# Second experts layer: weighted outputs summed slot by slot into the output, all shared tiles ahead of the slots

## The chip, the cores and the metric

The kernel runs as one program on one core of a Trainium2 chip. The metric is the device time of one execution in microseconds (us). Before the change the median of 3 runs is 1013.5 us (1013.17 to 1015.44). The profiled execution, from which all rows below come, took 1014.64 us, of which the trace spans 1012.9 us.

## The reference, cut to what matters

The program computes two layers, each cross attention followed by a mixture of experts, on 16 x 128 = 2048 tokens of 256 values. The change is in the last stage, the second mixture:

```python
shared = new_gelu(xf @ Wfc_s + bfc_s) @ Wproj_s + bproj_s
topk_p, topk_i = jax.lax.top_k(softmax(xf @ Wr), 2)
topk_p = topk_p / jnp.sum(topk_p, axis=-1, keepdims=True)
gate = jnp.zeros((N, 8)).at[jnp.arange(N)[:, None], topk_i].add(topk_p)
for e in range(8):
    h = new_gelu(xf @ Wfc[e] + bfc[e]) @ Wproj[e] + bproj[e]
    routed = routed + h * gate[:, e:e + 1]
x = x + shared + routed
```

Here xf is the layer norm of x, each expert has a hidden width of 1024, and each token goes to two of the eight experts. A shared expert of the same size takes every token. The first mixture has 14 experts of width 512 and no shared one.

## The kernel before

The kernel is written engine by engine: each engine's program is one list in the order in which the code is written, and semaphores tie the lists together. A stage ends with a barrier of all engines (`end_phase`). Tokens stand in 16 tiles of 128; `c["X"]` holds the running sum of all tiles in SBUF, `c["Hn"]` their layer norm.

**The stage `shared_expert`** does two things at once. TensorE takes tiles 0 to 13 (`SHARED_FIRST` = 14) through the shared expert: `turn` transposes a tile, `up` makes 8 chunks of 128 hidden values, `down` brings them back to 256 outputs, and VectorE adds these to X (L1698). Meanwhile VectorE builds the routing table: each of the 4096 pairs (token, expert) gets a place in one of 39 slots of 128 rows, where a slot belongs to one expert. `mark_places` and `mark_slots` write one-hot rows for each of 32 chunks, TensorE multiplies them in tiles 2 to 9 (L1432), and `slot_rows` turns the product into `src` (which token row a slot's row reads) and `dst` (where its output row goes). Rows of slots that no token fills read some row and write to a pad row. SyncE loads the weights of all eight experts, 16 MB, in this stage.

**The stage `experts`** runs over the 39 slots; it is used by both layers (45 slots in the first). GpSimd gathers a slot's 128 token rows with an indirect DMA (L1455), four slots ahead. TensorE transposes them, runs `up` for slot n+1, then `turn` for n+2, then `down` for n. VectorE copies the slot's first weights into the ring `wp` (L1924, two copies a slot in the second layer), copies the transposed rows (L1916), and adds the expert's bias to the output into `yb` (L1936). GpSimd scatters `yb` with an indirect DMA to the tensor `token_outputs` in HBM (L1776), where each pair has a row of its own. Slots 0 and 1 and the last ones are written out, the others run in a loop of two slots a turn.

**The end of the second layer.** After slot 38 TensorE takes the shared tiles 14 and 15 in the same pipeline (L1813, L1821, L1829). When all scatters have landed, SyncE loads for each tile the two rows of each token (L1759). VectorE multiplies both by the token's weights `w12` and adds them to X for tiles 0 to 9 (L1950, L1953); ScalarE multiplies (L1907) and GpSimd adds (L1797) for tiles 10 to 15. SyncE stores each tile to the output (L1765) and waits for all 16 stores.

Two orders matter below. On GpSimd the list is gather(n+4), scatter(n), with scatter waiting for `yb` and gather for a transpose. On VectorE each slot's bias add reads the expert's number into a register first, after the wait for the output:

```python
dve.wait_ge(y_done, n + 1)
if after(n, 2):
    dve.wait_ge(y_stored[par], 16 * k)
e = dve.value_load(routing["expert"][0:1, at(n)], min_val=0, max_val=E - 1)
```

Of the kernel before, what the change touches and what calls it, by code (L numbers as in the profile page):

```python
# [13 lines left out]
P = 128  # L14
B = 16
# [12 lines left out]
SHARED_FIRST = 14  # L28
CHUNK = 4
AHEAD = 4  # L30
ON_DVE = 10
LOAD_ORDER = (0, 10, 1, 2, 11, 3, 4, 12, 5, 6, 13, 7, 14, 8, 9, 15)
STORE_ORDER = (0, 1, 10, 2, 11, 3, 4, 12, 5, 13, 6, 7, 14, 8, 9, 15)
# [20 lines left out]
def build(nc, a, out):  # L54

    with ExitStack() as top:
# [39 lines left out]
        c["kv_stored"] = [nc.alloc_semaphore(f"kv_stored{i}") for i in range(2)]  # L96
        c["hn_stored"] = [nc.alloc_semaphore(f"hn_stored{layer}") for layer in range(2)]
# [34 lines left out]
        shared_expert(nc, sem, alloc, c, moe1, routing, weights, shared)  # L132
        end_phase()
        experts(nc, sem, alloc, c, moe1, routing, weights, shared, out)
# [1075 lines left out]
def table(keep, moe):  # L1210

    return {
        "w12": keep("w12", [P, B, TOPK]),
        "src": keep("src", [P, moe.slots], I32),
        "dst": keep("dst", [P, moe.slots], I32),
        "expert": keep("expert", [P, moe.slots], I32),
    }
# [56 lines left out]
def route_buffers(sb, moe, weights):  # L1274
# [3 lines left out]
    return {  # L1278
# [11 lines left out]
        "row": sb("row", [P, S]), "late": sb("late", [P, S]), "pad": sb("pad", [P, S]),  # L1290
    }

# [123 lines left out]
def mark_slots(dve, r, n, slot_ready):  # L1416

    j, b = place_chunks(r)[n]
    to = r["in_slot"][n % len(r["in_slot"])]
    for i in range(to.shape[1]):  # L1420
        last = dve.tensor_scalar(to[:, i], r["first_row"][:], r["start"][:, j, b + i:b + i + 1],
                                  r["code"][:, j, b + i:b + i + 1], ALU.is_equal, ALU.mult)
    last.then_inc(slot_ready, 1)
# [13 lines left out]
def slot_rows(dve, routing, r, T, inverted, made):  # L1437
# [9 lines left out]
    dve.tensor_tensor(r["pad"][:], r["pad"][:], r["row"][:], ALU.add).then_inc(made, 1)  # L1447
# [132 lines left out]
def shared_expert(nc, sem, alloc, c, moe, routing, weights, shared):  # L1580

    FC, N = moe.FC, SHARED_FIRST
    w1, w2 = shared["w1"], shared["w2"]
    with ExitStack() as stack:
# [9 lines left out]
        r["in_slot"] = [k[:].rearrange("p b e -> p (b e)")[:, 0:moe.slots].rearrange("p (o s) -> p o s", o=1)  # L1594
# [3 lines left out]
        slots_of = R[:, 2 * B * moe.E:2 * B * moe.E + moe.slots]  # L1598
# [95 lines left out]
        def _(dve):  # L1694
# [7 lines left out]
            for n in range(N):  # L1702
                if 2 <= n < 10:
                    for i in range(4 * (n - 2), 4 * (n - 1)):
                        mark_places(dve, r, i, start_ready, place_ready, inverted)
                        mark_slots(dve, r, i, slot_ready)
                if n == 10:
                    slot_rows(dve, routing, r, slots_of, inverted, made)
# [3 lines left out]
def experts(nc, sem, alloc, c, moe, routing, weights, shared=None, out=None):  # L1712
# [4 lines left out]
    n_all = n_slots if out is None else n_slots + B - SHARED_FIRST  # L1717
    CF = PIECE // P
    NP = moe.F // PIECE
    with ExitStack() as stack:  # L1720
# [21 lines left out]
        if out is not None:  # L1742

            yt = [weights["w1"][:, b * TOPK * D:(b + 1) * TOPK * D].rearrange("p (j d) -> p j d", j=TOPK) for b in range(B)]
            yt_got = [sem(f"yt_got{b}") for b in range(B)]
            routed_step, routed_added = sem("routed_step"), sem("routed_added")
            scaled, part_step, part_added, stored = sem("scaled"), sem("part_step"), sem("part_added"), sem("stored")
        block = stack.enter_context(nc.Block(no_gpsimd_drain=True))

        def tile_of(n):  # L1750
            return SHARED_FIRST + n - n_slots

        @block.sync
        def _(sp):
            if out is not None:
                for i in two:
                    sp.wait_ge(y_stored[i], 16 * ((n_slots + 1 - i) // 2))
                for b in LOAD_ORDER:
                    sp.dma_start(yt[b], token_outputs(c["yg"], b)).then_inc(yt_got[b], 16)  # L1759
                for b in STORE_ORDER:  # L1760
                    if b < ON_DVE:
                        sp.wait_ge(routed_added, b + 1)
                    else:
                        sp.wait_ge(part_added, b - ON_DVE + 1)
                    sp.dma_start(out[b], c["X"][:, b]).then_inc(stored, 16)  # L1765
                sp.wait_ge(stored, 16 * B)

        @block.gpsimd
        def _(pool):
# [4 lines left out]
            def scatter(n):  # L1774
                pool.wait_ge(y_ready, n + 1)
                pool.indirect_dma_start(out=c["yg"], out_offset=bass.IndirectOffsetOnAxis(  # L1776
                    ap=routing["dst"][:, n:n + 1].bitcast(U32), axis=0), in_=yb[n % 2][:], in_offset=None
                    ).then_inc(y_stored[n % 2], 16)

            for n in range(2, AHEAD):  # L1780
                gather(n)
            for n in range(n_slots):
                if n + AHEAD < n_slots:
                    gather(n + AHEAD)
                scatter(n)
            if out is None:
                for i in two:
                    pool.wait_ge(y_stored[i], 16 * ((n_slots + 1 - i) // 2))
            else:
                for b in range(ON_DVE, B):  # L1790
                    if b >= SHARED_FIRST:
                        pool.wait_ge(y_ready, n_slots + b - SHARED_FIRST + 1)
                    for j in two:
# [199 lines left out]
```

## Time and profile before

| what | value |
|---|---|
| median of 3 runs | 1013.5 us |
| profiled execution, its span | 1014.64 us, 1012.9 us |
| TensorE busy | 927.1 us, 92% |
| VectorE, ScalarE, GpSimd busy | 49%, 50%, 41% |
| second layer: tiles 0 to 13 | about 580 to 693 us |
| second layer: slots and tiles 14, 15 | about 694 to 997 us |
| last sums and stores | about 991 to 1012.9 us |

Times in a trace count from the start of the span. In the engine lists a row is a group of like instructions that follow one another: its start, its busy time, the engine, the line, the operation with output and input, the count, and in brackets the idle time in front of it with what ended it. A float32 matmul shows as two instructions. An indirect DMA's row on GpSimd is the time in which its descriptors are made; the transfer comes after it.

### The profile page before, as it was taken

The page shows a single profiled execution, that of the slowest core. Times are in us where ns is not written, and L with a number is a line of the kernel's source. Part 1 is how long each engine was busy: PE and PEld are TensorE (multiplying, and loading weights), DVE is VectorE, ACT ScalarE, POOL GpSimd, SP SyncE. Part 2 cuts the span into 40 slices and gives each one's busy share as a digit, 9 for nine tenths or more (in the row PEclk, how much of TensorE's full clock was granted, in tenths as well). Part 3 has the DMA queues.
Part 4 walks back from the last instruction along what each step waited for, and adds up shares of the span by engine and source line. Part 5 has one row for each costly group of instructions (what it writes and reads, how often), then busy time and mean ns, then how long its engine had stood idle before and what let it go on. Part 6 is the DMA issues. An engine that isn't in the chain of part 4 may idle for free. (4 is left out here: it accounts for less than half of the span.)

```text
span 1012.9 us, 25302 instructions
## 1 busy us (share of the span) xinstructions
PE 927.1 (92%) x7420; PEld 833.0 (82%) x7421; DVE 493.1 (49%) x2085; ACT 504.0 (50%) x1434; POOL 412.5 (41%) x534
## 2 busy tenths in 40 slices
PE   2799999688999999669999799998999999999993
PEld 2588888477999999647788599997999999999993
DVE  3588878654333343259999562212332323232315
ACT  2487778332333344259999453343434344343433
POOL 1877787301455555445665240001333333232314
PEclk9799999899999999869999799999999999999997
DMA  5866564187122222235221099000110111111107
GB/s 180 273 190 209 179 197 147 39 295 245 53 72 70 70 68 71 70 88 174 87 73 53 19 377 329 2 11 17 33 40 31 38 35 36 36 36 36 36 17 254
DMA packets 101322, 108.54 MB, mean 107 GB/s; under 512 B 9064, under 2 KB 87546, under 8 KB 100986
## 3 DMA queue, kind: packets, MB, share of 16 engines
q1 hardware_dynamic: 92272, 85.15, 26.1%
q0 software_dynamic: 8064, 22.03, 6.7%
q8 instruction: 40, 0.66, 0.3%
q10 hardware_dynamic: 906, 0.37, 0.1%
q14 instruction: 40, 0.33, 0.1%
HBM read 86.02 MB, written 21.50 MB: 106 GB/s over the span
## 5 line engine op out<-in xcount | busy, mean ns | idle before, releaser
L1844 PEld LDWEIGHTS experts_bank<-xT,wp 128*128 128x128 f32 x1968 | 236.4, 195 | 8.7 <-issue 4.6
L1844 PE MATMUL experts_bank<-xT,wp 128*128 128x128 f32 x1968 | 237.2, 278 | 4.0 <-DVE wp L1924 4.0
L1895 ACT ACTIVATE Hn<-experts_bank,vecT 128x128 f32<-128x128 f32 x312 | 114.3, 367 | 168.1 <-PE experts_bank L1844 146.5
L1776 POOL DMA_INDIRECT token_outputs<-yb,dst x84 | 95.1, 1132 | 215.2 <-DVE yb L1936 215.2
L1455 POOL DMA_INDIRECT rows<-token_rows,src x84 | 90.5, 1077 | 220.2 <-DVE dst L1450 119.4
L1854 PE MATMUL experts_bank<-w,Hn 128*128 x624 | 142.8, 382 | 0.0
L1936 DVE TENSOR_TENSOR yb<-experts_bank,b 128x256 f32<-128x256 f32 x84 | 35.7, 425 | 211.1 <-PE experts_bank L1854 211.1
L1924 DVE COPY wp<-w 128x1024 f32 x123 | 87.5, 712 | 96.7 <-PE experts_bank L1844 95.5
L1854 PEld LDWEIGHTS experts_bank<-w,Hn 128*128 128x128 f32 x624 | 115.4, 190 | 15.9 <-issue 0.2
L1895 ACT ACTIVATE hid<-experts_bank,vecT 128x128 f32<-128x128 f32 x180 | 65.6, 367 | 102.8 <-PE experts_bank L1854 77.6
L1854 PE MATMUL experts_bank<-w,hid 128*128 x360 | 85.0, 379 | 0.0
L1046 ACT ACTIVATE E<-U,mn 128x128 f32<-128x128 f32 x256 | 79.6, 392 | 3.2 <-DVE mn L1113 3.2
L596 ACT ACTIVATE E<-U,mn 128x128 f32<-128x128 f32 x256 | 79.8, 399 | 0.0
L383 POOL TENSOR_TENSOR fs<-fs,amb 128x1024 f32<-128x1024 f32 x32 | 75.7, 2367 | 0.3 <-DMA fs<-in_fside_Bx16xSxS_dram 0.3
L1854 PEld LDWEIGHTS experts_bank<-w,hid 128*128 128x128 f32 x360 | 65.0, 190 | 7.0
L1679 ACT ACTIVATE hid<-shared_bank,vecT 128x128 f32<-128x128 f32 x112 | 41.0, 367 | 56.8 <-PE shared_bank L1638 49.8
L1113 DVE CUSTOM_DVE_ANT_0 U<-attn_bank,M 128x128 f32<-128x128 f32 x256 | 57.8, 287 | 7.8 <-PE attn_bank L928 7.6
L665 DVE CUSTOM_DVE_ANT_0 U<-attn_bank,fs 128x128 f32<-128x128 f32 x256 | 57.5, 285 | 6.3 <-PE attn_bank L470 6.1
L1638 PE MATMUL shared_bank<-xT,w_shared 128*128 128x128 f32 x448 | 54.1, 281 | 0.0
L1638 PEld LDWEIGHTS shared_bank<-xT,w_shared 128*128 128x128 f32 x448 | 52.8, 196 | 0.2
L1647 PE MATMUL shared_bank<-w_shared,hid 128*128 128x256 f32 x224 | 50.5, 379 | 0.0
L1647 PEld LDWEIGHTS shared_bank<-w_shared,hid 128*128 128x128 f32 x224 | 41.5, 190 | 5.1
(266 smaller groups left out, 1461.6 us busy)
## 6 DMA issues: line engine op xcount, KB each, us to landing
fs<-in_fside_Bx16xSxS_dram SPq DMA_DIRECT2D x32, 512.0 KB, 4.4
w<-in_L_ffn_w_dram SPq DMA_DIRECT2D x28, 512.0 KB
w<-in_L_ffn_Wfc_dram SPq DMA_DIRECT2D x8, 1024.0 KB, 13.8
w<-in_L_ffn_Wproj_dram SPq DMA_DIRECT2D x8, 1024.0 KB, 12.6
ctx<-in_ctx_dram SPq DMA_DIRECT2D x32, 128.0 KB, 4.9
token_rows<-Hn SPq DMA_DIRECT2D x32, 128.0 KB, 3.1
keys_values<-WT SPq DMA_DIRECT2D x16, 256.0 KB, 3.8
y<-token_outputs SPq DMA_DIRECT2D x16, 256.0 KB, 3.2
```

The lines of the kernel that those rows point to most:

```text
L383: pool.tensor_tensor(fs[b % 2][:, heads], fs[b % 2][:, heads], bcast(amb[:, b:b + 1], [P, 8, P]), ALU.add).then_inc(bias_ready[half], 1)
L596: last = act.activation(E_[:, h], U[:, h], ACT.Exp, bias=mn[b % 2][:, h:h + 1], scale=-1.0)
L1046: last = act.activation(E_[:, h], U[:, h], ACT.Exp, bias=mn[b % 2][:, h:h + 1], scale=-1.0)
L1113: last = dve.tensor_tensor_reduce(U[:, h], scores_of(h), c["M1"][:], -1.0, BIG, ALU.add, ALU.min, mn[b % 2][:, h:h + 1])
L1455: pool.indirect_dma_start(out=weights["rows"][:, n % 2], out_offset=None, in_=c["hn"], in_offset=bass.IndirectOffsetOnAxis(ap=routing["src ...
L1638: last = pe.matmul(HB[f % 4][:, 0:P], w1[:, i, f * P:(f + 1) * P], xT[n % 2][:, i], start=(i == 0), stop=(i == DC - 1))
L1647: last = pe.matmul(Y[n % 2][:, 0:D], hid[n % 2][:, f], w2[:, f], start=(f == 0), stop=(f == FC - 1))
L1776: pool.indirect_dma_start(out=c["yg"], out_offset=bass.IndirectOffsetOnAxis(ap=routing["dst"][:, n:n + 1].bitcast(U32), axis=0), in_=yb[n ...
L1844: last = pe.matmul(HB[f % 4][:, 0:P], piece[:, i, (f % CF) * P:(f % CF + 1) * P], xT[par][:, i], start=(i == 0), stop=(i == DC - 1))
L1854: last = pe.matmul(Y[par][:, 0:D], hid[par][:, f], weights["w2"][:, bass.ds(e * (FC * D) + f * D, D)], start=(f == 0), stop=(f == FC - 1))
L1895: act.activation(hid[par][:, f], HB[f % 4][:, 0:P], moe.act, bias=bias).then_inc(hid_ready, 1)
L1924: dve.tensor_copy(wp[par if NP == 1 else q][:], of[:, :, q * PIECE:(q + 1) * PIECE]).then_inc(wp_ready, 1)
```

## The change

1. `shared_expert` takes all 16 tiles. SyncE stores each finished tile of X to the output, behind the weight loads. Tiles 14 and 15 and their code are gone from `experts`.
2. The one-hot rows of `mark_slots` are twice as wide in this stage: 39 columns for the row code and 39 for the pair's weight, so the same product also gives each slot row its weight, kept in the new table `share`.
3. With `summed=True`, `dst` is the token's own row. Unfilled slot rows point beyond the last row and are left out by the bound of the DMA, which is held in a register.
4. In `experts` of the second layer GpSimd has a third indirect DMA in each slot, `get_sums(n)`: it reads the current output rows of the slot's tokens, once scatter(n-1) has landed. VectorE adds the bias to `yb`, waits for these sums, and makes `yb` = `yb` x share + sums. The scatter writes that back to the output rows. The two buffers of the sums are X's tiles 0 and 1.
5. The loads of `token_outputs`, the weighted sums on three engines and the 16 stores at the end are gone. The end now waits for the last two scatters.
6. The read of the expert's number stands ahead of the wait for the output, in both layers.

```diff
+            for b in range(B):
+                sp.wait_ge(y_added, b + 1)
+                sp.dma_start(out[b], c["X"][:, b]).then_inc(c["x_stored"], 16)
...
+        if w12 is not None:
+            last = dve.tensor_scalar(to[:, i, S:2 * S], r["first_row"][:], r["start"][:, j, b + i:b + i + 1],
+                                     w12[:, b + i, j:j + 1], ALU.is_equal, ALU.mult)
...
-    FC, N = moe.FC, SHARED_FIRST
+    FC, N, S = moe.FC, B, moe.slots
...
-                sp.wait_ge(stored, 16 * B)
...
+            def get_sums(n):
+                if n == 0:
+                    pool.wait_ge(c["x_stored"], 16 * B)
+                else:
+                    pool.wait_ge(y_stored[(n - 1) % 2], 16 * ((n - 1) // 2) + 16)
+                pool.indirect_dma_start(out=sums[n % 2], out_offset=None, in_=token_sums, in_offset=bass.IndirectOffsetOnAxis(
+                    ap=routing["dst"][:, n:n + 1].bitcast(U32), axis=0), bounds_check=last_row, oob_is_err=False
+                    ).then_inc(sums_got[n % 2], 16)
...
             for n in range(n_slots):
+                if out is not None:
+                    get_sums(n)
                 if n + AHEAD < n_slots:
                     gather(n + AHEAD)
                 scatter(n)
...
-                dve.wait_ge(y_done, n + 1)
-                if after(n, 2):
-                    dve.wait_ge(y_stored[par], 16 * k)
                 e = dve.value_load(routing["expert"][0:1, at(n)], min_val=0, max_val=E - 1)
...
+                    share = routing["share"][:, at(n)]
+                    dve.wait_ge(y_done, n + 1)
+                    if after(n, 2):
+                        dve.wait_ge(y_stored[par], 16 * k)
+                    dve.tensor_tensor(yb[par][:], Y[par][:, 0:D], b2, ALU.add).then_inc(biased, 1)
+                    dve.wait_ge(biased, n + 1)
+                    dve.wait_ge(sums_got[par], 16 * k + 16)
+                    dve.scalar_tensor_tensor(yb[par][:], yb[par][:], share, sums[par], ALU.mult, ALU.add
+                                             ).then_inc(y_ready, 1)
```

GpSimd's list at the first slots of the second layer, before (`rows` are gathered token rows, `token_outputs<-yb` is the scatter):

```order
L1455 DMA rows<-token_rows,src 128x256 x3
L1776 DMA token_outputs<-yb_398,dst 9856x256
L1455 DMA rows<-token_rows,src 128x256
L1776 DMA token_outputs<-yb_399,dst 9856x256
L1455 DMA rows<-token_rows,src 128x256
```

and now (`X<-out_dram,dst` is get_sums, `out_dram<-yb` the scatter):

```order
L1462 DMA rows<-token_rows,src 128x256 x2
L1780 DMA X<-out_dram,dst 128x256
L1462 DMA rows<-token_rows,src 128x256
L1772 DMA out_dram<-yb_398,dst 2048x256
L1780 DMA X<-out_dram,dst 128x256
L1462 DMA rows<-token_rows,src 128x256
L1772 DMA out_dram<-yb_399,dst 2048x256
L1780 DMA X<-out_dram,dst 128x256
```

Between two scatters there is now a read of the output rows, and the gather stands behind it.

VectorE's list in the loop of the second layer, one slot, before (TENSOR_LOAD reads the expert's number; the ISA rows L1934 and L1935 are the waits for the output and for the buffer):

```order
L1916 COPY xT_395<-experts_bank 128x256
L1934 ISA
L1935 ISA
L1935 TENSOR_LOAD expert
L1935 ISA x2
L1936 ISA
L1936 TENSOR_TENSOR yb_398<-experts_bank,b_336 128x256
```

and now:

```order
L1870 COPY xT_395<-experts_bank 128x256
L1886 ISA
L1886 TENSOR_LOAD expert
L1886 ISA x2
L1897 ISA
L1898 ISA
L1898 TENSOR_TENSOR yb_398<-experts_bank,b_337 128x256
L1900 REGISTER_ALU
L1901 REGISTER_ALU
L1901 SCALAR_TENSOR_TENSOR yb_398<-yb_398,share,X 128x256
```

The read of the number stands ahead of the waits (L1897, L1898), and the weighted sum is behind the bias add.

## Rows read from the trace of the kernel before

**Rows 1.** Busy time by stretch: from:to, length, PE, PEld, DVE, ACT, POOL, clock, DMA, GB/s

```profile
712.00:970.00 258.00, 258.00 (x1766) 241.57 (x1765) 78.11 (x142) 104.02 (x284) 79.74 (x69) 1.00 0.11 36
```

**Rows 2.** Chain that ended last: start, us, what; two slots apart

```profile
877.38 3.57 PE experts_bank L1844 x32
...
892.00 3.57 PE experts_bank L1844 x32
```

**Rows 3.** Engine list of TensorE at the end

```profile
975.98 3.62 PE L1854 MATMUL experts_bank<-w,Hn 128*128 x16
979.43 3.73 PE L1821 MATMUL experts_bank<-xT,w_shared 128*128 128x128 f32 x32
...
990.25 7.07 PE L1829 MATMUL experts_bank<-w_shared,Hn 128*128 128x256 f32 x32
```

**Rows 4.** Engine list, SyncE's queue at the end

```profile
990.71 9.02 SPq L1759 DMA_DIRECT2D w<-token_outputs  x16
999.76 10.71 SPq L1765 DMA_DIRECT2D out_dram<-X  x16
```

**Rows 5.** Waits of SyncE's queue, 985 us to the end: total, times, longest

```profile
SPq L1720 <- DMA out_dram<-X: 1.4, 1, 1.4
```

**Rows 6.** Engine list of GpSimd and VectorE: last scatter; a slot in mid stage

```profile
988.30 0.97 POOL L1776 DMA_INDIRECT token_outputs<-yb,dst  x1 [6.27 <-DVE yb L1936]
...
820.46 1.34 POOL L1776 DMA_INDIRECT token_outputs<-yb,dst  x1 [3.54 <-DVE yb L1936]
...
820.98 0.69 DVE L1924 COPY wp<-w 128x1024 f32 x1 [0.80 <-PE experts_bank L1844]
...
822.97 1.19 POOL L1455 DMA_INDIRECT rows<-token_rows,src  x1 [1.17 <-PE experts_bank L1807]
```

**Rows 7.** Line L1455, the gathers from 712 to 960 us: ns min/median/max

```profile
L1455 POOL DMA_INDIRECT rows<-token_rows,src x34: 1187/1192/1199, 713.3 to 954.5; - x34
...
DMA to landing us min/median/max: 2.9/3.0/3.8
```

**Rows 8.** DMA traffic from 822 to 828 us, in 40 slices of 0.15 us

```profile
GB/s 0 0 273 437 164 0 0 0 0 0 0 0 0 0 0 0 0 0 0 328 55 328 109 55 0 0 0 0 0 0 0 0 0 0 0 0 0 0 0 0
```

**Rows 9.** Engine list of VectorE: weighted sums, alone and beside GpSimd's adds

```profile
994.76 0.48 DVE L1953 SCALAR_TENSOR_TENSOR X<-w,w,X 128x256 f32<-128x256 f32 x1
...
1006.82 1.04 DVE L1950 SCALAR_TENSOR_TENSOR X<-w,w,X 128x256 f32<-128x256 f32 x1
```

**Rows 10.** Engine list at the end of the first layer's slots

```profile
419.04 3.62 PE L1854 MATMUL experts_bank<-w,hid 128*128 x16
...
423.43 0.42 DVE L1936 TENSOR_TENSOR yb<-experts_bank,b 128x256 f32<-128x256 f32 x1 [1.31 <-PE experts_bank L1854]
...
424.13 0.97 POOL L1776 DMA_INDIRECT token_outputs<-yb,dst  x1 [0.76 <-DVE yb L1936]
```

**Rows 11.** Engine list from the last shared tile to the first slot

```profile
689.75 2.75 PE L1647 MATMUL shared_bank<-w_shared,hid 128*128 128x256 f32 x12
...
692.54 0.42 DVE L1698 TENSOR_TENSOR X<-X,shared_bank 128x256 f32<-128x256 f32 x1 [3.03 <-PE shared_bank L1647]
...
693.87 0.63 PE L1807 MATMUL experts_bank<-ident,rows 128*128 128x128 f32 x4 [1.37 <-PEq L69]
```

**Rows 12.** Engine list of TensorE, shared tiles 11 and 12

```profile
674.61 3.73 PE L1638 MATMUL shared_bank<-xT,w_shared 128*128 128x128 f32 x32
...
681.86 3.73 PE L1638 MATMUL shared_bank<-xT,w_shared 128*128 128x128 f32 x32
```

**Rows 13.** Engine list in a shared tile with routing: VectorE, TensorE

```profile
625.99 0.42 DVE L1698 TENSOR_TENSOR X<-X,shared_bank 128x256 f32<-128x256 f32 x1 [6.07 <-PE shared_bank L1647]
...
626.52 0.30 DVE L1421 TENSOR_SCALAR hot<-first_row,start,code 128x39 f32<-128x39 f32 x1
...
625.92 0.39 PE L1432 MATMUL shared_bank<-hot,pre 128*128 128x39 f32 x2
626.15 0.39 PE L1432 MATMUL shared_bank<-tmp,both 128*128 128x39 f32 x2
```

More of the change, by code:

```diff
@@ L131, in build @@
         expert_w1(alloc(top), moe1, weights)
-        shared_expert(nc, sem, alloc, c, moe1, routing, weights, shared)
+        shared_expert(nc, sem, alloc, c, moe1, routing, weights, shared, out)
         end_phase()
-        experts(nc, sem, alloc, c, moe1, routing, weights, shared, out)
+        experts(nc, sem, alloc, c, moe1, routing, weights, out)
         end_phase()
@@ L1216, in table @@
         "expert": keep("expert", [P, moe.slots], I32),
+        "share": keep("share", [P, moe.slots]),
     }
@@ L1289, in route_buffers @@
         "pad_row": sb("pad_row", [P, S]), "place": sb("place", [P, TOPK, B]), "start": sb("start", [P, TOPK, B]),
-        "row": sb("row", [P, S]), "late": sb("late", [P, S]), "pad": sb("pad", [P, S]),
+        "row": sb("row", [P, S]), "late": sb("late", [P, S]),
     }
+    r["pad"] = r["expf"]
+    return r
 def route_counters(pool, r, iotas_ready):
@@ L1446, in slot_rows @@
     dve.wait_ge(made, 2)
-    dve.tensor_tensor(r["pad"][:], r["pad"][:], r["row"][:], ALU.add).then_inc(made, 1)
+    dve.tensor_tensor(r["pad"][:], r["pad"][:], r["late" if summed else "row"][:], ALU.add).then_inc(made, 1)
     dve.tensor_copy(routing["src"][:], r["late"][:])
@@ L1577, in _, with shared_expert @@
             slot_rows(dve, routing, r, T, inverted, made)
-def shared_expert(nc, sem, alloc, c, moe, routing, weights, shared):
-    FC, N = moe.FC, SHARED_FIRST
+def shared_expert(nc, sem, alloc, c, moe, routing, weights, shared, out):
+    FC, N, S = moe.FC, B, moe.slots
     w1, w2 = shared["w1"], shared["w2"]
@@ L1742, in experts @@
         if out is not None:
[L1744 to L1747, printed above, removed]
+            token_sums = out.rearrange("b p d -> (b p) d")
+            sums = [c["X"][:, i] for i in two]
+            sums_got, biased = [sem(f"sums_got{i}") for i in two], sem("biased")
         block = stack.enter_context(nc.Block(no_gpsimd_drain=True))
[L1750 to L1765, printed above, removed]
-                sp.wait_ge(stored, 16 * B)
         @block.gpsimd
@@ L1785, in _ @@
                 scatter(n)
[L1786 to L1793, printed above, removed]
-                        pool.wait_ge(scaled, TOPK * (b - ON_DVE) + j + 1)
-                        if j == 1:
-                            pool.wait_ge(part_step, b - ON_DVE + 1)
-                        pool.tensor_tensor(c["X"][:, b], c["X"][:, b], yt[b][:, j], ALU.add
-                                           ).then_inc(part_added if j == 1 else part_step, 1)
+            for i in two:
+                pool.wait_ge(y_stored[i], 16 * ((n_slots + 1 - i) // 2))
         @block.tensor
@@ L1876, in _ @@
             paired(pe, n_slots, slot)
-            for n in range(n_slots, n_all):
-                slot(n, n % 2, n // 2)
         @block.scalar
@@ L1896, in _ @@
             paired(act, n_slots, slot)
-            for n in range(n_slots, n_all):
-                act.wait_ge(y_done, n - 1)
-                for f in range(FC):
-                    act.wait_ge(hid_done, FC * n + f + 1)
-                    act.activation(hid[n % 2][:, f], HB[f % 4][:, 0:P], moe.act, bias=c["vecT1"][:, 64 + f:65 + f]
-                                   ).then_inc(hid_ready, 1)
-            if out is not None:
-                for b in range(ON_DVE, B):
-                    act.wait_ge(yt_got[b], 16)
-                    for j in two:
-                        act.activation(yt[b][:, j], yt[b][:, j], ACT.Copy, scale=routing["w12"][:, b, j:j + 1]
-                                       ).then_inc(scaled, 1)
         @block.vector
```

94 lines of the change are left out of this document (30 added, 64 removed).

## The prediction, as it was recorded

> **What bounds the kernel now.** I read the busy times by stretch first. From 712 to 970 us, the slots of the second layer, TensorE is busy for 258.00 of 258.00 us, VectorE for 78, GpSimd for 80, and the DMA engines for 0.11 of their time [rows 1]. The reader is to see that nothing but TensorE's own list costs time there. The chain of waits says the same: one slot's matmuls follow the last one's, and two slots take 892.00 - 877.38 = 14.62 us, so a slot takes P = 7.31 us [rows 2]. The engine lists of the last 40 us show where that ends. The output of slot 37 is done at 975.98 + 3.62 = 979.60 us, then TensorE still has tiles 14 and 15 until 997.32 us [rows 3]. From 990.71 us SyncE loads the two outputs of each token and from 999.76 us stores the sums, the last issue ending at 1010.47 us [rows 4]. So the end is bound by loads, sums and stores, some 15 us of it behind TensorE's last matmul.
>
> **What the change takes away at the end.** I follow slots 37 and 38 on the clock of the kernel before. After 979.60 us TensorE no longer has a tile's `up` in front of `down(38)`, so slot 38 is done about 3.5 us later, at 983.1 us.
> - Slot 37's bias add starts at once at about 979.65 and takes 0.42 [rows 10]; the weighted sum takes 0.48 [rows 9]. It is done at 980.58.
> - GpSimd starts a scatter 0.28 us after VectorE is done (424.13 - 423.43 - 0.42) [rows 10], at 980.86.
> - A scatter has landed and woken its waiter 990.71 - 988.30 = 2.41 us after its start [rows 4, 6]. get_sums(38) starts at 983.27.
> - The nearest row to get_sums is the gather, of the same 128 rows of 1 KB from HBM: 3.0 us to landing [rows 7]. That this counts from the start of the issue shows in the traffic: the gather of 822.97 [rows 6] has its bytes moved between 824.85 and 825.6 [rows 8], 2.6 us after its start. So the sums are there at 986.27.
> - Slot 38's own output and bias are ready by 983.6, so the sums are last. The weighted sum ends at 986.8, the scatter starts at 987.06 and has landed at 989.5.
> - The kernel before ends its last issue at 1010.47 [rows 4], waits 1.4 us [rows 5], and its span ends at 1012.9, 1.0 us after that. I take the same 1.0: 990.5.
>
> The end thus comes 1012.9 - 990.5 = 22.4 us earlier on that clock.
>
> **What it adds ahead of the slots.** Two more tiles in `shared_expert`, without routing work, at 681.86 - 674.61 = 7.25 us each [rows 12]: +14.5. The last tile's store must be issued before SyncE reaches the barrier. The barrier took from 692.96 to 693.87 before [rows 11]. A store's issue takes 0.56 to 0.67 us in the groups of 16 (9.02 and 10.71 over 16) [rows 4], of which all lies behind the last add: +0.5 to +0.7, I take +0.5 as the last group's total holds waits. The other 15 stores are issued under later tiles.
>
> The read of the expert's number now comes before the wait. Before, the last bias add of the first layer started at 423.43, 0.77 us after TensorE's end at 422.66 [rows 10]; an add without such a read started 0.04 after TensorE (692.50, 692.54) [rows 11]. In the slots this lies beside TensorE's work, but the last slot of the first layer ends its stage, whose barrier waits for the scatter: -0.7. A failure of this term costs just these 0.7. The same move is worth nothing extra in the second layer beyond the instant start already counted.
>
> Sum: -22.4 + 14.5 + 0.5 - 0.7 = -8.1 us.
>
> **What it adds and I cost at nothing.**
> - Routing: one more VectorE operation of at most 0.30 us for each of 32 chunks, 1.2 us in each of eight tiles where VectorE idles 6.07 [rows 13]. Without that cover it would be 9.6 us. The product has 78 columns for 39. A pair of instructions with 39 columns starts 0.23 us after the last, 0.115 each [rows 13], and those with 128 columns take 3.73/32 = 0.117 [rows 12]. 78 lies between, so 0.
> - In each slot: one weighted sum of 0.48 us on VectorE, 19 us over 39 slots against 180 idle in the 258 us; one more issue of about 1.2 us on GpSimd, 47 us against 178 idle [rows 1]; 128 KB more to read.
> - The pad rows left out make transfers smaller; I count 0.
>
> **The wait that is added.** Slot n's sums cannot be read before slot n-1's are written, so the slots get a loop of their own: weighted sum, scatter, landing, read, landing. Its time is C = 0.48 + 0.28 + 2.41 + 3.0 = 6.2 us alone. In mid stage a scatter's issue takes up to 1.34 for 0.97, when a `wp` copy of VectorE runs beside it (820.98) [rows 6], so 6.5. The gather's 3.0 has such a copy in it already, its issue being 1.19 [rows 7]. Against P = 7.31 some 0.8 us are left in each slot, and the loop stays hidden. Behind get_sums(n) on GpSimd stand gather(n+4), which has two slots of time, and scatter(n), which waits for get_sums anyway. Behind the weighted sum on VectorE stand the `wp` copies for slot n+3: 0.69 + 0.69 and 0.42 for the transposed rows, needed a slot later, so a delay of the sum by 3 us stops nobody, once.
>
> C is bounded thus: from below 0.48 + 0.28 + 2.41 + 2.9 = 6.07; from above, with every maximum in every slot, 1.04 + 0.28 + 2.78 + 3.8 = 7.9 [rows 6, 7, 9]. As soon as C is over P, each slot is paced by it: 38 (C - 7.31) more. The upper end gives 38 x 0.59 = +22 us, that is 1027.9. The maxima of the gather are single ones (the median is 3.0), so I stay at 6.5. No row shows an indirect DMA with a bound. It may be cheaper, as rows are left out, or dearer. The row with the same engine and shape says 1.19 us for one issue, and I add nothing.
>
> A copy beside an issue costs 0.37 us here [rows 6], half of the copy. The Trainium skill (SBUF — State Buffer, Who interferes with whom) says that GpSimd is fully blocked for the whole of a VectorE operation in a two-port mode once that has started. By that rule each of the two issues could wait for a whole copy, which the third rival prices from rows.
>
> **The rivals.**
> 1. The loop decides by a large price of the bound (slower). The bound is tested for each of 128 rows by the engine that makes the descriptors; the issue has 0.97 us for all of them. If each of the two issues in the loop takes x more, C = 6.5 + 2x. From x = 0.4 on it paces the slots, and from 2x = 0.81 + 8.1/38, x = 0.51, the kernel is slower than before. With x = 0.7, C = 7.9 and the time is 1027.9. For it: no row has this form, the margin is thin. Against: it would be over half of the present issue, for one compare with a register in each row.
> 2. The landing of the scatter is slower when the sums are read from the rows just written, or mean landings lie toward the 3.8 of [rows 7]. C between 7.35 and 7.5: +1.5 to +7, about 1009.
> 3. The copies block each issue for their whole 0.69 us. C = 0.48 + 0.28 + 2.41 + 0.69 + 3.0 + 0.47 (the gather has 0.22 of it) = 7.33. That is P: 38 x 0.02 = +0.8, about 1006. The row with 0.37 speaks against it. It is what the rule of the Trainium skill named above would make of this loop at most.
> 4. The tail is shorter than I count, since the last DMAs have no copies beside them and land at 2.9 or less, twice: some 1 us less, 1004.
>
> **How the numbers follow.** The change is -8.1 against the profiled execution's span, 1012.9 to 1004.8, and its own time, 1014.64 to 1006.5. That execution took 1.1 us more than the median of the runs; against the median it is 1013.5 - 8.1 = 1005.4 us. I give 0.68 to the forecast with its own range of 1003.4 to 1007.5 (rivals 3 and 4 lie in it), 0.03 to less, 0.16 to rival 2 (1007.5 to 1012) and 0.13 to rival 1, above. From 0.2% on (2.0 us, what a measurement of this kernel can tell) it is faster below 1011.5 and slower above 1015.5: faster 0.68 + 0.03 + 0.11 = 0.82, same 0.05, slower 0.13. The range for 8 in 10 takes the forecast's own and most of rival 2: 1003 to 1011.
>
> **What the profile of the changed kernel would show.** TensorE busy for the whole of the slots, at 7.31 us a slot, says the loop is hidden; idle time of TensorE in front of L1844's successor or of `down`, and VectorE's weighted sum waiting for the DMA in each slot, says it isn't. The weighted sum should wait for VectorE's own bias add in mid stage, and for the DMA only at slot 38. GpSimd's issues of get_sums near 1.2 us say that the bound is free. The last scatter should start 8 to 9 us after slot 37's output, and the span should end some 3.4 us after that. The first layer's last scatter should start 0.7 us nearer to TensorE's end. A time above 1011.5 us would make the prediction wrong.

## The result, and the profile after

The changed kernel takes 1006.12 us (median of 7 runs, 1005.75 to 1010.36) against 1013.79 us for the kernel before on the same chip. The ratio is 0.9928, with a 95% interval of 0.9916 to 0.9940: 7.7 us faster. Forecast were 1005.4 us and -8.1. The profiled execution took 1005.75 us, its span is 1004.1, 8.8 less than before.

The busy times by stretch of the changed kernel, in the columns of [rows 1]:

```profile
712.00:970.00 258.00, 258.00 (x1769) 242.13 (x1769) 93.11 (x175) 105.28 (x287) 109.02 (x104) 1.00 0.17 50
970.00:1004.00 34.00, 26.28 (x171) 24.14 (x169) 7.99 (x16) 8.81 (x24) 10.31 (x10) 0.95 0.03 5
```

TensorE is still busy for the whole of the slots. VectorE has 15 us more than in [rows 1], GpSimd 29 and the DMA engines 0.17 for 0.11, all of it in idle time. So the slots' own loop is hidden.

Who waited for whom from 700 us to the end (total, times, longest), and the line of the sums' reads (ns min/median/max):

```profile
POOL X L1780 <- DMA out_dram<-yb,dst: 62.1, 37, 1.8
...
DVE yb L1901 <- DVE yb L1898: 3.6, 17, 0.2
DVE yb L1901 <- DMA X<-out_dram,dst: 3.4, 1, 3.4
...
L1780 POOL DMA_INDIRECT X<-out_dram,dst x39: 1013/1021/1223, 711.1 to 998.1; - x39
...
DMA to landing us min/median/max: 2.1/2.8/3.0
```

GpSimd waits for the scatter's landing in nearly each slot, as its list makes it. The weighted sum waits for its sums once in 39 slots, at the very end. A read with a bound has an issue of 1.02 us; in the same loop the gathers without one take 0.97.

One slot in mid stage, GpSimd and VectorE:

```profile
833.15 0.48 DVE L1901 SCALAR_TENSOR_TENSOR yb<-yb,share,X 128x256 f32<-128x256 f32 x1
833.91 1.28 POOL L1772 DMA_INDIRECT out_dram<-yb,dst  x1 [1.94 <-DVE yb L1901]
...
836.89 1.02 POOL L1780 DMA_INDIRECT X<-out_dram,dst  x1 [1.70 <-DMA out_dram<-yb,dst]
838.22 0.97 POOL L1462 DMA_INDIRECT rows<-token_rows,src  x1 [0.30 <-issue]
...
840.09 0.42 DVE L1898 TENSOR_TENSOR yb<-experts_bank,b 128x256 f32<-128x256 f32 x1 [2.90 <-PE experts_bank L1829]
840.73 0.48 DVE L1901 SCALAR_TENSOR_TENSOR yb<-yb,share,X 128x256 f32<-128x256 f32 x1 [0.21 <-DVE yb L1898]
```

From the sum's start to the scatter it is 0.76 us, from there to the read of the next sums 2.98, and a read lands after 2.8 in the median: C = 6.54 us (6.4 in the mean of all slots). This read landed after 2.5 us, at 839.4, and is wanted at 840.7. That slot is one of the roomier ones. The weighted sums stand 7.05 and 7.57 us apart in turn, so the time between the landing of the sums and their use is about 0.7 us in one slot and 1.0 or more in the next; the least is 0.6. The forecast had 0.8 in each.

The end of the changed kernel, all engines:

```profile
989.21 7.07 PE L1829 MATMUL experts_bank<-w,Hn 128*128 x32
989.60 1.02 POOL L1780 DMA_INDIRECT X<-out_dram,dst  x1 [1.40 <-DMA out_dram<-yb,dst]
992.97 0.42 DVE L1898 TENSOR_TENSOR yb<-experts_bank,b 128x256 f32<-128x256 f32 x1 [6.08 <-PE experts_bank L1829]
...
994.20 1.03 POOL L1772 DMA_INDIRECT out_dram<-yb,dst  x1 [3.59 <-DVE yb L1901]
...
998.05 1.02 POOL L1780 DMA_INDIRECT X<-out_dram,dst  x1 [2.82 <-issue]
1000.27 0.48 DVE L1901 SCALAR_TENSOR_TENSOR yb<-yb,share,X 128x256 f32<-128x256 f32 x1 [3.42 <-DMA X<-out_dram,dst]
1001.03 1.04 POOL L1772 DMA_INDIRECT out_dram<-yb,dst  x1 [1.96 <-DVE yb L1901]
```

Against [rows 3, 4] the loads and stores are gone, and the chain of slots 37 and 38 ends the span. One thing in it was not forecast: the chain of waits puts the scatter's landing at 996.35 us, but get_sums(38) starts at 998.05, with nothing that GpSimd waited for ("issue"). That pause is taken up below.

The seam before the slots and the end of the first layer's slots:

```profile
705.94 0.42 DVE L1708 TENSOR_TENSOR X<-X,shared_bank 128x256 f32<-128x256 f32 x1 [3.03 <-PE shared_bank L1657]
707.76 0.63 PE L1804 MATMUL experts_bank<-ident,rows 128*128 128x128 f32 x4 [1.86 <-PEq L65]
...
418.75 3.62 PE L1829 MATMUL experts_bank<-w,hid 128*128 x16
422.51 0.42 DVE L1892 TENSOR_TENSOR yb<-experts_bank,b 128x256 f32<-128x256 f32 x1 [1.30 <-PE experts_bank L1829]
423.21 0.97 POOL L1769 DMA_INDIRECT token_outputs<-yb,dst  x1 [0.76 <-DVE yb L1892]
```

From the last add's end to the first transpose it is 1.40 us, for 0.91 in [rows 11]. From TensorE's end (422.37) to the last bias add it is 0.14 us, for 0.77 in [rows 10].

### The profile page after: what moved, and what is told of

Its sections match the earlier page's. It is cut to its first block and busy times, and to the rows that moved or that the text cites. A ratio compares the mean times of both kernels' runs of the same rounds, so it can differ in the third digit from the quotient of the medians.

```text
span 1004.1 us, 25421 instructions
## 1 busy us (share of the span) xinstructions
PE 928.6 (92%) x7420; PEld 834.4 (83%) x7421; DVE 507.2 (51%) x2135; ACT 499.4 (50%) x1424; POOL 437.5 (44%) x561
## 5 line engine op out<-in xcount | busy, mean ns | idle before, releaser
L1462 POOL DMA_INDIRECT rows<-token_rows,src x84 | 82.6, 983 | 198.4 <-DVE dst L1457 119.2
L1772 POOL DMA_INDIRECT out_dram<-yb,dst x39 | 45.7, 1172 | 88.0 <-DVE yb L1901 88.0
L1689 ACT ACTIVATE hid<-shared_bank,vecT 128x128 f32<-128x128 f32 x128 | 46.9, 367 | 64.8 <-PE shared_bank L1648 56.7
L1769 POOL DMA_INDIRECT token_outputs<-yb,dst x45 | 51.5, 1144 | 61.4 <-DVE yb L1892 61.4
L1898 DVE TENSOR_TENSOR yb<-experts_bank,b 128x256 f32<-128x256 f32 x39 | 16.6, 425 | 110.4 <-PE experts_bank L1829 110.4
L1780 POOL DMA_INDIRECT X<-out_dram,dst x39 | 40.4, 1035 | 65.2 <-DMA out_dram<-yb,dst 62.1
L1648 PE MATMUL shared_bank<-xT,w_shared 128*128 128x128 f32 x512 | 61.2, 280 | 0.0
L1648 PEld LDWEIGHTS shared_bank<-xT,w_shared 128*128 128x128 f32 x512 | 60.2, 196 | 0.3
```

The source lines that it names most:

```text
L1462: pool.indirect_dma_start(out=weights["rows"][:, n % 2], out_offset=None, in_=c["hn"], in_offset=bass.IndirectOffsetOnAxis(ap=routing["src ...
L1648: last = pe.matmul(HB[f % 4][:, 0:P], w1[:, i, f * P:(f + 1) * P], xT[n % 2][:, i], start=(i == 0), stop=(i == DC - 1))
L1769: pool.indirect_dma_start(out=c["yg"], out_offset=at_rows, in_=yb[n % 2][:], in_offset=None).then_inc(y_stored[n % 2], 16)
```

## The experiments

Theory: the gain is the old end (loads, sums, stores) less the two tiles moved ahead, and the slots' loop costs nothing because it is shorter than TensorE's slot. Rivals: the order of the tiles is the gain; the loop has no room; the bound or GpSimd's load costs.

**One part alone: all tiles first, old end.** An edit of the kernel before:

```diff
-SHARED_FIRST = 14
+SHARED_FIRST = 16
...
-                add_tile(n_slots)
...
-                add_tile(n_slots + 1)
```

> The kernel before with one part of the change alone: all 16 shared tiles ahead of the slots, the old end kept (loads of both outputs, weighted sums, stores). My account: two tiles move ahead (+14.5), and the last slot's output comes 4.5 us earlier than the kernel before had it, but the loads and sums, 22.2 us from the first load to the end of the span, lose the cover of two tiles. Loads start at 986.9 on the old clock, end at 1008.3 (two adds of 0.42 are gone), plus 14.5: span 1022.8, which is +9.9 over the kernel before, about 1023.5 us. Rival: most of the gain of the change comes from the order of the tiles: then this is near or under 1013.5.

Measured: 1024.39 us, ratio to the kernel before 1.0104 (1.0090 to 1.0117): 10.5 us slower than 1013.89 beside it. Its queue of SyncE at the end:

```profile
999.61 9.01 SPq L1759 DMA_DIRECT2D w<-token_outputs  x16
1008.66 10.40 SPq L1765 DMA_DIRECT2D out_dram<-X  x16
```

From the first load to the end of the span (1021.5) it is 21.9 us, for 22.2 before. So the tile order by itself loses what the cover was worth, and the rest of the change brings 18 us, the difference of 1024.4 and 1006.1. Nearly all of that is the slot-wise sums; 0.6 is the earlier read of the number in the first layer.

**The loop lengthened by one issue.** The extra DMA reads 128 rows into an unused tile:

```diff
                     pool.wait_ge(y_stored[(n - 1) % 2], 16 * ((n - 1) // 2) + 16)
+                one_more(n)
                 pool.indirect_dma_start(out=sums[n % 2],
...
```

> The changed kernel with one more indirect DMA in each slot, a read of 128 token rows into a buffer that nobody uses, issued between the landing of the scatter and the read of the sums, so inside the slots' own loop. My account: the loop takes 6.5 us of the 7.31 that TensorE needs for a slot. One more issue puts 1.0 and the 0.3 between two issues into it, and the transfer in front of the sums' another 0 to 0.3: C = 7.8 to 8.1, and 38 slots times 0.5 to 0.8 is +19 to +30 us: 1025 to 1036. The weighted sums then wait for the DMA in each slot and TensorE idles. Rival: the loop is much shorter than I count, or the 3 us of room on VectorE take up the delay: same time as the changed kernel within 2 us.

Measured: 1028.51 us, ratio 1.0137 (1.0122 to 1.0153). Its weighted sum, in the list of waits and in the trace:

```profile
DVE yb L1911 <- DMA X<-out_dram,dst: 155.0, 38, 5.8
...
901.46 0.48 DVE L1911 SCALAR_TENSOR_TENSOR yb<-yb,share,X 128x256 f32<-128x256 f32 x1 [4.43 <-DMA X<-out_dram,dst]
...
909.22 0.48 DVE L1911 SCALAR_TENSOR_TENSOR yb<-yb,share,X 128x256 f32<-128x256 f32 x1 [4.54 <-DMA X<-out_dram,dst]
...
904.96 0.96 POOL L1779 DMA_INDIRECT X<-token_rows,src  x1 [1.72 <-DMA out_dram<-yb,dst]
906.22 1.02 POOL L1788 DMA_INDIRECT X<-out_dram,dst  x1 [0.30 <-issue]
```

Now the sum waits for the DMA in 38 of 39 slots. Over the stage the scatters stand 7.81 us apart in the mean, and a scatter and the next read of the sums 4.07 us, for 2.88 in the changed kernel: +1.19. So the loop of the changed kernel takes 7.81 - 1.19 = 6.6 us, the C of the forecast. From the first scatter to the last it is 296.6 us, for 276.9 in the changed kernel, so 19.7 of the 22 us lie in the slots. The end costs the same in both (3.0 us from the last scatter). What is left is no more than runs differ by ahead of this stage, where the code is the same: the first shared tile starts at 585.9 us in this trace, at 579.8 in that of the changed kernel and at 583.6 in another one below.

**The same DMA beside the loop.**

```diff
                 if out is not None:
                     get_sums(n)
+                    one_more(n)
```

> The same extra indirect DMA in each slot, issued behind the read of the sums, so beside the loop: GpSimd has 1.9 us more between the gather and the next scatter. My account: cost 0 to 1 us, as GpSimd and the DMA engines are idle there: 1006 to 1007. Rival: it is the load of GpSimd or of its DMA queue that costs, wherever the DMA stands: then as slow as the kernel with the issue inside the loop.

Measured: 1004.13 us, ratio 0.9898 (0.9882 to 0.9913). No cost, on the same chip as the last one. GpSimd was busy for 141.64 of the 258 us from 712 to 970. Load on GpSimd or its queue is not what costs; the place in the loop is. That it came out 2 us under the changed kernel has a likely cause in the pause (below): from scatter(37) to the end of the span it takes 8.4 us, for 9.9.

**Half a dose in the loop.** A memset of GpSimd, about half as long as an issue, takes the place of the extra DMA:

```diff
                     pool.wait_ge(y_stored[(n - 1) % 2], 16 * ((n - 1) // 2) + 16)
+                    pool.wait_ge(filled, n - 1)
+                    pool.memset(unused[:], 0.0).then_inc(filled, 1)
```

> The changed kernel with a GpSimd memset of 128x512 (0.5 us) in each slot between the landing of the scatter and the read of the sums. My account: one whole issue there (1.2 us more from scatter to read) made the loop 7.80 us, so the loop of the changed kernel takes 6.6 and has 0.7 of room under 7.31. The memset uses 0.5 to 0.6 of it: no cost in the slots. Only the end pays, where the loop is on the chain once: +0.5 us, about 1006.6. Rival: there is no room, and the extra issue cost because the loop already sat at TensorE's time: then 38 times 0.5, +19 us, 1025.

Measured: 1007.82 us (1004.91 to 1009.56), ratio 0.9941 (0.9922 to 0.9960). Its slots, in the columns of [rows 1]:

```profile
712.00:970.00 258.00, 258.00 (x1768) 241.85 (x1768) 92.80 (x175) 104.73 (x286) 130.57 (x137) 1.00 0.17 50
```

From scatter to read of the sums it now takes 3.46 us in the mean for 2.88, and TensorE does not idle. There is room for 0.58 us more in the loop and not for 1.19. The dose takes nearly all of it: in every second slot the sums now land only 0.18 us before the weighted sum starts, and in some of these it waits for them.

**The number read late again.**

```diff
+                dve.wait_ge(y_done, n + 1)
+                if after(n, 2):
+                    dve.wait_ge(y_stored[par], 16 * k)
                 e = dve.value_load(routing["expert"][0:1, at(n)], min_val=0, max_val=E - 1)
...
-                    dve.wait_ge(y_done, n + 1)
-                    if after(n, 2):
-                        dve.wait_ge(y_stored[par], 16 * k)
...
```

> The changed kernel with one thing undone: the expert's number is again read behind the wait for the output, in both layers. My account: it costs only where the bias add ends a stage or feeds the chain that ends last. First layer's last slot: the bias add starts 0.77 us after TensorE's end for 0.14 now, +0.6. Second layer: slot 37's weighted sum, +0.7. In the slots between nothing. Sum +1.3 us, about 1007.4 against 1006.1. Rival: the read was also hurting each slot of the own loop (weighted sum, scatter, read of the sums), so that its return pushes the loop over 7.31 us a slot: +5 us or more, with TensorE idle between slots.

Measured: 1007.39 us, ratio 0.9934 (0.9920 to 0.9947). The time does not tell it from the changed kernel (0.9928), the trace does:

```profile
422.02 3.62 PE L1829 MATMUL experts_bank<-w,hid 128*128 x16
...
426.42 0.42 DVE L1894 TENSOR_TENSOR yb<-experts_bank,b 128x256 f32<-128x256 f32 x1 [1.31 <-PE experts_bank L1829]
...
992.99 7.07 PE L1829 MATMUL experts_bank<-w,Hn 128*128 x32
997.37 0.42 DVE L1896 TENSOR_TENSOR yb<-experts_bank,b 128x256 f32<-128x256 f32 x1 [6.07 <-PE experts_bank L1829]
```

0.78 us behind TensorE's end in the first layer for 0.14, and in slot 37 4.38 us from the start of `down` to the bias add for 3.76: 0.6 each.

**The last store a stage later.** SyncE issues the store of tile 15 as the first thing of the slots' stage:

```diff
-            for b in range(B):
+            for b in range(B - 1):
                 sp.wait_ge(y_added, b + 1)
                 sp.dma_start(out[b], c["X"][:, b]).then_inc(c["x_stored"], 16)
...
+        @block.sync
+        def _(sp):
+            if out is not None:
+                sp.dma_start(out[B - 1], c["X"][:, B - 1]).then_inc(c["x_stored"], 16)
```

> The changed kernel with the store of tile 15 issued by SyncE as the first thing of the slots' stage instead of the last thing of the shared stage. My account: the barrier no longer waits for the issue; VectorE's last add to TensorE's first transpose goes from 1.40 back to the 0.91 of the kernel before: -0.5 us, 1005.6. Rival: the seam is 0.5 longer for another reason (the longer stage code, the copies): no change, or slower because get_sums(0) waits for the later landing.

Measured: 1005.29 us, ratio 0.9912 (0.9896 to 0.9927). The changed kernel, run again beside it, gave 1007.62 us, ratio 0.9933 (0.9916 to 0.9950), so the time alone does not decide. The trace does. Its seam:

```profile
706.33 0.42 DVE L1708 TENSOR_TENSOR X<-X,shared_bank 128x256 f32<-128x256 f32 x1 [3.03 <-PE shared_bank L1657]
...
707.66 0.63 PE L1809 MATMUL experts_bank<-ident,rows 128*128 128x128 f32 x4 [1.36 <-PEq L65]
```

0.91 us, as in the kernel before. The 0.5 us of the seam were the issue of that store.

The trace shows a second gain that was not expected, in the first slots. First the changed kernel, then this one: the first 64 matmuls of `up`, and the stretch from 710 to 714 us in the columns of [rows 1].

```profile
710.10 9.01 PE L1819 MATMUL experts_bank<-xT,wp 128*128 128x128 f32 x64 [1.71 <-DVE wp L1878]
710.00:714.00 4.00, 3.90 (x20) 3.93 (x21) 0.81 (x2) 1.36 (x4) 1.79 (x2) 0.57 0.33 98
...
710.09 7.38 PE L1824 MATMUL experts_bank<-xT,wp 128*128 128x128 f32 x64 [1.81 <-DVE wp L1883]
710.00:714.00 4.00, 3.91 (x35) 3.94 (x36) 1.24 (x2) 2.57 (x7) 1.78 (x2) 1.00 0.33 94
```

In the changed kernel the granted clock of TensorE falls to 0.5, which is 1.2 GHz, at 710.4 us for 3.4 us. TensorE had stood idle for 1.86 and 1.71 us before that, with four short instructions between. With the store moved it idles 1.36 and 1.81 us, and the clock stays at 1.00, which is 2.4 GHz, for all of the slots. That is worth another 1.6 us (9.01 - 7.38). In the two traces with this store moved (this one and that of the last version below) the clock stays, in the eleven others it falls there. That the shorter seam keeps it up is not shown: the kernel with all tiles first and the old end has the same seam (0.91, idle for 1.37 and 1.71 us), and its clock falls. So 0.5 us are the store's, and the 1.6 are seen with it, with an open cause. Together they make 2.1 in the trace; the two medians stand 2.3 apart, with intervals that overlap. The kernel before has the same 3.4 us at 0.5, from 697.9 us (behind 1.37 and 2.06 us of idle time), so this is no part of the 7.7 us of the change.

**The bound.** This kernel keeps the sums in `token_outputs`, where unfilled rows have rows of their own, and leaves out the output itself, for which it stores one unrelated tile. It has 40 more stores of 128 KB in the shared stage.

```diff
-            token_sums = out.rearrange("b p d -> (b p) d")
+            token_sums = c["yg"]
...
-                    ap=routing["dst"][:, n:n + 1].bitcast(U32), axis=0), bounds_check=last_row, oob_is_err=False
+                    ap=routing["dst"][:, n:n + 1].bitcast(U32), axis=0)
```

> The changed kernel without the bound: the sums are kept in token_outputs, where rows of a slot that no token fills have rows of their own again, so nothing is left out of any transfer. It leaves out the output itself (one unrelated tile is stored in its place). SyncE has 40 more stores of 128 KB in the shared stage, beside TensorE's work. My account: the bound costs 0.05 us an issue (reads of the sums take 1.02, gathers 0.97) and saves the transfer of unfilled rows, so in the slots nothing changes; at the end, slots 37 and 38, which no token fills, now move their bytes: landings of 2.1 become 2.6 to 3.0 us, three of them on the chain: +1 to +2.5 us, and the extra store at the seam +0.4. 1008 to 1010. Rival: the bound itself is a cost in the loop: then this kernel is faster, and the issues fall by more than 0.1 us.

Measured: 1008.18 us, ratio 0.9937 (0.9913 to 0.9961). Its reads of the sums:

```profile
L1783 POOL DMA_INDIRECT X<-token_outputs,dst x39: 949/972/1193, 712.4 to 999.7; - x39
...
DMA to landing us min/median/max: 2.6/2.7/3.0
```

0.97 us an issue for 1.02: the bound costs 0.05 us, and the loop nothing. From scatter(37) to the end of the span this kernel takes 11.0 us (995.60 to 1006.6) for 9.9. Here the last two slots move their bytes: the two scatters land after 2.43 and 2.46 us and the read between them after 2.75, for 2.15, 2.17 and 2.12 in the changed kernel.

**The pause in front of the last read.** In the changed kernel scatter(37) and get_sums(38) stand 3.85 us apart, those of the slot before 2.43. It stands so in the second run of it too:

> The changed kernel itself, as the yardstick for the three runs beside it: 1006.1 us within 1 us, and the 1.4 us pause of GpSimd in front of the last read of the sums (3.85 us from scatter(37) to get_sums(38), against 2.4 for the slot before) again in its trace.

```profile
993.55 1.03 POOL L1772 DMA_INDIRECT out_dram<-yb,dst  x1 [3.59 <-DVE yb L1901]
997.40 1.02 POOL L1780 DMA_INDIRECT X<-out_dram,dst  x1 [2.82 <-issue]
```

My first idea was a place in GpSimd's instruction list, since the pause had left the last read in the two kernels with one more DMA a slot. I put four tiny instructions ahead:

> The changed kernel with four tiny GpSimd instructions (8 numbers each into an unused buffer) at the start of the slots, 90 slots' worth of instructions ahead of the pause. Theory: the pause of 1.4 us in front of get_sums(38) belongs to a place in GpSimd's instruction stream (it stood elsewhere in the two kernels with one more DMA in each slot, and at the same place in the kernel with the number read late, whose GpSimd list is the same). Shifting the list by four instructions moves it out of the last slot into time in which GpSimd waits anyway: -1.4 us, about 1004.7. Rival: the pause belongs to the last read itself (its scatter or its landing): then it stays, and the time is 1006.1.

Measured: 1005.63 us, ratio 0.9911 (0.9896 to 0.9926), and from scatter(37) to get_sums(38) still 3.86 us. The idea of the place fell. Counting then showed that in each kernel the pause stands in front of the 206th indirect DMA of the execution. With one more DMA a slot it is a scatter near slot 27. In the kernel with that DMA beside the loop:

```profile
925.72 1.01 POOL L1773 DMA_INDIRECT out_dram<-yb,dst  x1 [2.15 <-issue]
```

The next run puts two more indirect DMAs at the start of the slots, where GpSimd is idle, and so moves the count by two:

```diff
+                for i in two:
+                    pool.indirect_dma_start(out=c["X"][:, 2 + i], out_offset=None, in_=c["hn"], in_offset=bass.IndirectOffsetOnAxis(
...
```

> The changed kernel with two more indirect DMAs (reads of token rows into unused tiles) once, behind the first read of the sums, where GpSimd is idle. In all eight traces with slot-wise sums the pause of GpSimd stands in front of the 206th indirect DMA of the execution, whatever that one is: get_sums(38) in those with 207 in all, a scatter near slot 27 in those with 246. Theory: the pause belongs to the count of indirect DMAs. With two more the 206th is get_sums(37), which has some 1.7 us of room; scatter(37) to get_sums(38) falls from 3.85 to 2.4 us and the time by 1.4 us, against the changed kernel 1005.5 or so (its medians were 1006.1 and 1007.6). Rival: it belongs to the last read; then the 3.85 stays and the time too.

Measured: 1005.35 us, ratio 0.9905 (0.9886 to 0.9924).

```profile
989.15 1.03 POOL L1773 DMA_INDIRECT out_dram<-yb,dst  x1 [2.70 <-DVE yb L1908]
991.87 1.02 POOL L1781 DMA_INDIRECT X<-out_dram,dst  x1 [1.69 <-DMA out_dram<-yb,dst]
996.18 1.03 POOL L1773 DMA_INDIRECT out_dram<-yb,dst  x1 [3.29 <-DVE yb L1908]
998.59 1.03 POOL L1781 DMA_INDIRECT X<-out_dram,dst  x1 [1.38 <-DMA out_dram<-yb,dst]
```

The last read now follows its scatter by 2.41 us. So the pause goes with the count of indirect DMAs. At the 206th, now get_sums(37), only 0.3 us of it show (2.72 for 2.43). The kernel with the half dose has a memset in front of its 206th:

```profile
995.50 0.52 POOL L1782 MEMSET unused<- 128x512 f32 x1 [1.17 <-DMA out_dram<-yb,dst]
997.19 1.03 POOL L1783 DMA_INDIRECT X<-out_dram,dst  x1 [1.17 <-issue]
```

The memset starts on time, and the DMA starts 1.17 us behind its end, for 0.15 in the slot before. So GpSimd still ran a memset there, and what came late is the DMA's issue. What happens at that place, and why its length differs, stays open. The time fell by 0.8 to 2.3 us against the two medians of the changed kernel, with intervals that overlap, so the 1.4 us are shown in the trace and not in the time.

**A version that beats both.** The sums slot by slot, but tiles 14 and 15 behind the slots again, as cover for the chain of the last slots. The last store of the shared stage, now that of tile 13, is also issued a stage later, as above:

```diff
-    FC, N, S = moe.FC, B, moe.slots
+    FC, N, S = moe.FC, SHARED_FIRST, moe.slots
...
+                b = SHARED_FIRST - 1
+                sp.dma_start(out[b], c["X"][:, b]).then_inc(c["x_stored"], 16)
+                for i in two:
+                    sp.wait_ge(y_stored[i], 16 * ((n_slots + 1 - i) // 2))
+                sp.dma_start(c["X"][:, SHARED_FIRST:B], out.rearrange("b p d -> p b d")[:, SHARED_FIRST:B]).then_inc(back, 16)
+                for b in range(SHARED_FIRST, B):
+                    sp.wait_ge(tile_added, b - SHARED_FIRST + 1)
+                    sp.dma_start(out[b], c["X"][:, b]).then_inc(stored, 16)
```

> A further version: slot-wise sums as in the changed kernel, but tiles 14 and 15 of the shared expert again behind the slots. Their rows of the output start as X with the bias; when the last scatter has landed SyncE reads both tiles back, VectorE adds the shared outputs, SyncE stores them. The last store of the shared stage is also issued a stage later. My account: TensorE's work is the same, so it ends at 995.8 on the changed kernel's clock (0.5 less for the seam); the chain of slots 37 and 38 (7 us) and the read back (3 us) then lie beside the tiles; after TensorE come 0.5 for the add, 1.9 for the store's landing and 1.0 to the end: 999.2 against 1004.1, so -4.9: 1001.2 us. Rival: the read back is late and the add of tile 14 waits for it, or the stores collide: -2 or less.

Measured: 1000.93 us (999.54 to 1003.26), ratio 0.9859 (0.9841 to 0.9877), where the changed kernel beside it has 0.9933.

```profile
985.82 1.02 POOL L1803 DMA_INDIRECT X<-out_dram,dst  x1 [2.82 <-issue]
...
991.25 7.07 PE L1849 MATMUL experts_bank<-w_shared,Hn 128*128 128x256 f32 x32
991.40 0.39 SPq L1776 DMA_DIRECT2D X<-out_dram  x1
994.98 0.42 DVE L1974 TENSOR_TENSOR X<-X,experts_bank 128x256 f32<-128x256 f32 x1 [6.04 <-PE experts_bank L1849]
995.43 3.71 SPq L1779 DMA_DIRECT2D out_dram<-X  x2
998.36 0.42 DVE L1974 TENSOR_TENSOR X<-X,experts_bank 128x256 f32<-128x256 f32 x1 [2.96 <-PE experts_bank L1849]
```

The pause and the last reads lie beside TensorE's tiles, both adds wait for TensorE alone, and the span ends 3.2 us after its last matmul (1001.5, 998.32). In the changed kernel these are 7.8 us.

The gain over the changed kernel is 6.7 us against the run beside it, where 4.9 were expected. The traces divide it: 0.5 at the seam are the later store's, 1.6 lie in the first `up` (7.38 us for 9.01), where the clock does not fall, and about 4.8 come with the two tiles behind the slots (14.4 less ahead of them, 9.6 more behind). The clock was not in the expectation.

## Why the prediction was right

The terms of the sum, on the two profiled executions:

| term | forecast | measured | from |
|---|---|---|---|
| the end, from the start of down(37) | -22.4 | -22.0 | 1012.9 - 975.98, 1004.1 - 989.21 |
| two tiles and the seam | +15.0 | +14.9 | first shared to first slot transpose: 113.10, 128.01 |
| first layer's last scatter | -0.7 | -0.6 | TensorE's end to the next stage's first load: 4.68, 4.09 |
| slots of the second layer | 0 | -0.7 | first slot transpose to down(37): 282.11, 281.45 |
| all else, which the change does not touch | 0 | -0.4 | the rest of -8.8 |

**The end** was right within 0.4 us, but by luck: two errors went against each other. The chain from slot 37's output to the end of the span was forecast at 10.9 us and took 11.3. The read of the last sums was forecast at 3.0 us to the weighted sum and took 2.2, and the last scatter was forecast at 3.4 us to the end of the span and took 3.0, which makes -1.2. No token fills these slots, and the bound leaves their rows out: the DMA queues show 0.00 MB from 983 to 1004 us. I had counted that at 0, and the kernel without the bound, with its bytes moved, shows what it is worth. From scatter(37) to the read it was forecast at 2.41 us, which the slot before has (2.43), and took 3.85: the pause of 1.4 us, which no row of before showed, took the gain back.

One sign of the forecast does not follow from its own chain. The chain has the last scatter 7.5 us after slot 37's output (979.60 to 987.06), the list of signs says 8 to 9. Measured were 8.2 (992.83 to 1001.03), which is in that range only because of the pause. The fourth rival, a shorter tail by 1 us, had the size right and the cause wrong: it named the copies, not the missing bytes.

**The loop** was forecast at 6.5 us and measured at 6.5 from the rows and 6.6 from the lengthened one. It stayed hidden, which was the step on which the sign hung. The rival of the dear bound needed 0.5 us an issue and found 0.05. The rival of slower landings fell with the median of 2.8 for the reads, and 2.88 us in the mean from a scatter to the next read. The rival of the blocking copies: an issue with a copy beside it takes up to 1.22 for 1.02 and 1.34 for 1.03, so 0.2 to 0.3 us and not 0.69. The Trainium skill (SBUF — State Buffer, Who interferes with whom) has GpSimd blocked for the whole of a VectorE instruction in a two-port mode that started first. In this case's traces less than half of the copy shows in the issue, 0.31 of 0.69 us at most.

**The read of the number** brought 0.6 for 0.7, as 0.14 us are still left between TensorE's end and the add, where an add without such a read had 0.04 [rows 11]. **The seam** was 0.5, and the run with the later store shows it to be the issue of tile 15's store. The forecast had nothing on TensorE's clock behind the seam, and needed nothing, as both kernels have the same 3.4 us at 0.5. **The routing work** cost nothing, as the stage's length shows.

The -0.7 in the slots was not forecast: 0.35 of it is an earlier first `wp` copy (1.50 us after the first transpose for 1.85), the rest is not explained. It is under what runs of one kernel differ by, so I draw nothing from it.

## What to carry to other kernels

A serial loop of dependent DMAs (write, read back, add) costs nothing as long as its time from landing to landing is under the bound engine's time for one item, and everything over it is paid in each item. Work it out from landings and issues, and test its room with a dose or two before relying on it; here 0.6 us fitted, just, and 1.2 did not. Moving work ahead of a loop is no gain by itself, since it can be the cover of the end: when the end has become a short chain, put the independent work back behind it. Read the granted clock behind a seam between two stages before you credit an edit there: here 0.5 us were the edit's, and 1.6 more went with 3.4 us at half the clock that were or were not there.

## What was not expected of the hardware

GpSimd paused in front of the 206th indirect DMA of the execution in each kernel with slot-wise sums, by some 1.4 us where it was on the chain. It moved with their count and not with four instructions of another kind, and a memset of GpSimd's in front of it was on time. Indirect DMAs of which every row lies outside the bound still take 1.02 us to issue and 2.1 to 2.2 us to land; with all their bytes, at the same place, a read took 2.75 and a scatter 2.4 to 2.5.
